# A fused transformer stack: VectorE's statistics cut into single instructions between the scan's steps, PE's and GpSimd's jobs moved to other steps, filler matmuls taken out

## The reference, cut to what matters

```python
def _L0_tok_ref(...):
    emb = tok_table[token_ids] + seg_table[segment_ids] + pos_table[:seq_len][None, :, :]
    ...
    out = (emb - mu) * jax.lax.rsqrt(var + EPS) * gamma + beta

def selective_scan(z, W_xproj, W_dt, b_dt, A_log, D_skip):
    ...
    A_bar = jnp.exp(dt[..., None] * A)
    Bx = (dt * z)[..., None] * Bm[:, :, None, :]
    ...
    _, h = jax.lax.associative_scan(comb, (A_bar, Bx), axis=1)   # h = A_bar * h + Bx along a sequence
    y = jnp.einsum('blds,bls->bld', h, Cm) + D_skip * z

def _L0_attn_ref(x, ...):
    h = rmsnorm(x, w_norm1)
    z = h @ W_in.T
    z = z * jax.nn.sigmoid(h @ W_gate.T)
    y = selective_scan(z, W_xproj, W_dt, b_dt, A_log, D_skip)
    x = residual + y @ W_out.T
    hf = rmsnorm(x, w_ffn_norm)
    return x + jax.nn.silu(hf @ W_gate_ffn.T) * (hf @ W_up.T) @ W_down.T
...
h = _L0_tok_ref(...)
h = h + _L0_attn_ref(_layernorm(h), ...)
h = h + _L0_ffn_ref(_layernorm(h), ...)     # router and 8 experts
```

## Time and profile before

| | us |
|---|---|
| median of three runs | 1750.38 |
| the three runs | 1747.45, 1750.38, 1765.43 |
| the profiled execution, its own time | 1742.62 |
| its span | 1740.9 |
| scan stage in it, first multiply to last scan's end (96.1 to 617.5) | 521.4 |

### The profile page before, as it was taken

The page is one execution under the profiler, slowest core; times in us unless marked ns, Lnnn a source line. Parts: engine busy times, 40 slices in busy tenths (PEclk is TensorE's granted clock), DMA queues, the critical chain, the costliest instruction groups (busy, mean ns, idle before and its releaser), DMA issues.

```text
span 1740.9 us, 23318 instructions
## 1 busy us (share of the span) xinstructions
PE 1355.9 (78%) x7240; PEld 943.2 (54%) x7240; DVE 817.2 (47%) x1505; ACT 520.3 (30%) x878; POOL 519.9 (30%) x418
## 2 busy tenths in 40 slices
PE   0567678889988874699993778989998889998960
PEld 0223333243254453699883554756657488888850
DVE  2478887777688764011112726355453422222212
ACT  0453444764734410133231313315150101001000
POOL 6366644745654471000003400000001600000025
PEclk9978888888798886899997768898988899999985
DMA  5064433433443313889982100000000388888843
GB/s 126 19 167 113 110 89 85 126 98 85 120 105 85 73 53 111 250 274 274 263 260 73 43 1 1 1 1 0 0 1 10 121 226 239 227 233 236 226 128 95
DMA packets 71614, 206.44 MB, mean 119 GB/s; under 512 B 11360, under 2 KB 32608, under 8 KB 66752
## 3 DMA queue, kind: packets, MB, share of 16 engines
q1 hardware_dynamic: 59648, 181.28, 37.9%
q0 software_dynamic: 11904, 24.40, 4.8%
HBM read 183.42 MB, written 22.22 MB: 118 GB/s over the span
## 4 chain that ended last, share of the span: by engine, by line
PE 35%; DMA 24%; DVE 14%; issue 11%; POOL 6%; POOLq 4%; ACT 2%; DVEq 2%; SPq 1%; ACTq 1%
PE ps L825 22%; DMA expert<-arena 21%; PE ps L956 4%; DVE arena L1498 3%; PE ps L1197 3%; POOL arena L545 2%; PE ps L970 1%; PE ps L986 1%; DMA arena<-sorted 1%; DVE ps L1493 1%; POOLq L536 1%; PE ps L1189 1%; POOL ew_out L454 1%; PE ps L820 1%; ACT arena L787 1%
## 5 line engine op out<-in xcount | busy, mean ns | idle before, releaser
L1498 DVE TENSOR_TENSOR_SCAN arena<-arena,ps 128x1024 f32<-128x1024 f32 x96 | 219.6, 2287 | 25.8 <-ACT arena L686 12.8
L825 PE MATMUL ps<-arena 96*128 96x128 f32 (+1 forms) x1680 | 222.8, 290 | 9.9 <-issue 8.3
L825 PEld LDWEIGHTS ps<-arena 96*128 96x128 f32 (+1 forms) x1680 | 213.6, 191 | 14.7 <-issue 14.5
L825 PE MATMUL ps<-xTF,wreg 96*128 96x512 f32 x352 | 207.1, 736 | 8.8 <-DVE arena L1675 5.0
L533 POOL DMA_DIRECT2D expert<-arena x88 | 47.7, 542 | 493.9 <-DVE arena L1635 270.5
L956 PE MATMUL ps<-arena,pick 32*128 32x512 f32 x384 | 124.6, 739 | 86.9 <-DVE arena L1498 75.3
L412 POOL DMA_INDIRECT sorted<-x_rows,row_i x64 | 63.0, 985 | 409.1 <-DVEq L1414 390.4
L825 PE MATMUL ps<-arena,ew_in 96*128 96x128 f32 x1248 | 150.0, 278 | 8.1 <-issue 7.7
L825 PEld LDWEIGHTS ps<-arena,ew_in 96*128 96x128 f32 x1248 | 145.6, 194 | 11.9 <-issue 11.9
L454 POOL TENSOR_TENSOR ew_out<-arena 128x1024 f32<-128x1024 f32 x48 | 112.6, 2351 | 107.4 <-DVE arena L1498 56.6
L1493 DVE TENSOR_TENSOR ps<-ps,arena 128x1024 f32<-128x1024 f32 x96 | 117.2, 1221 | 58.3 <-PE ps L956 56.3
(11 more groups left out here) (213 smaller groups left out, 1867.8 us busy)
## 6 DMA issues: line engine op xcount, KB each, us to landing
arena<-dt SPq DMA_DIRECT2D x64, 512.0 KB, 4.6
ew_in<-in_e_in SPq DMA_DIRECT2D x24, 768.0 KB, 6.1
arena<-in_e_in SPq DMA_DIRECT2D x24, 768.0 KB, 6.1
ew_in<-dt SPq DMA_DIRECT2D x32, 512.0 KB, 4.8
ew_out<-in_e_out SPq DMA_DIRECT2D x20, 675.0 KB, 6.9
arena<-in_e_out SPq DMA_DIRECT2D x20, 675.0 KB, 7.1
ew_in<-in_e_in SPq DMA_DIRECT2D x20, 576.0 KB, 5.5
arena<-in_e_in SPq DMA_DIRECT2D x20, 576.0 KB, 5.6
```

The source lines that it names most:

```text
L825: last = pe.matmul(o, lhs, rhs, start=(n == 0), stop=(n == len(pairs) - 1))
L1498: ve.tensor_tensor_scan(hid[k % 3], dec[k % 3], bx.rearrange("p x t -> p (x t)"), 0.0, ALU.mult, ALU.add)\
```

## The change

The functions `leave_rms` and `leave_norm`, and the calls of `embed_norm` and `embed_rows` in the scan stage, go. The same instructions stand in two new functions. `tile_work` holds what works on whole tiles (`bn_stats`, and the scaling of embedded rows), two tiles at a time behind a scan. `small_work` holds all the rest as 167 pieces of one instruction (`bn_aggr` of four tiles, and one pair, count as one piece); a step has 5 places for pieces in chunks 0 and 3 and 3 in chunks 1 and 2. The first place lies between the multiply and the scan, the others behind the scan; each piece has a `drain` ahead of it. `keep_busy` goes with all its 120 matmuls. The tables of PE's and ScalarE's jobs are written anew, GpSimd's side jobs move to other steps (the residual add from 11, 12 to 5, 6; the embedding of chunks 2 and 3 has a semaphore each and is spread differently), and the bias of the scores of chunk 2 comes behind the loop. The code after the scan stage is the same.

```diff
-        leave_late = {3: [("lnext", 0), ("lnext", 1)], 6: [("lrout", 0)], 7: [("lrout", 1)], 8: [("lscore", 0)]}
+        leave_late = {0: [("ldown", 1)], 8: [("lnext", 0), ("lnext", 1)], 9: [("lrout", 0)], 10: [("lrout", 1)], 11: [("lscore", 0)]}
...
-                    if c and n in (11, 12):
-                        add_mamba(c - 1, n - 11)
+                    if c and n in (5, 6):
+                        add_mamba(c - 1, n - 5)
...
-            def keep_busy(c, n, todo):
...
-                units = 7 - 2 - (2 if n % 2 else 0) - sum(cost[job[0]] for job in todo)
...
-                for _ in range(units):
-                    pe.matmul(ps[:, b, 0:2 * P], ident, cst[:, 0:2 * P], start=True, stop=True)
...
-                keep_busy(c, n, todo)
...
-            def leave_rms(c):
-                ve.wait_ge(s_mr, 2 * (c + 1))
-                moments(mr, CT)
-                rstd(l_rms[:, :], CT, RMS_EPS, True)
-                ve.drain().then_inc(s_rr, 1)
...
+            def root_part(i, o, eps, out):
+
+                v, h, y, t = [w[:, o:o + CT] for w in (vv, vh, yy, tt)]
+                if i == 0:
+                    ve.tensor_scalar(v, mv[:, o:o + CT, 1], eps, None, ALU.add)
+                elif i == 1:
+                    ve.tensor_scalar(ti[:, o:o + CT], v.bitcast(I32), 1, None, ALU.logical_shift_right)
+                    ve.tensor_scalar(h, v, -0.5, None, ALU.mult)
...
+                elif i % 3 == 0:
+                    ve.tensor_tensor(t, y, y, ALU.mult)
...
+            def slots(c):
+                return 3 if c in (1, 2) else 5
+
+            def small_work(c, n, x):
+
+                at = n * slots(c) + x
+                s = slots(c)
...
+                def drained(first, parts):
+                    ve.drain()
+                    return here(first, parts)
+
+                if c == 0:
+                    if here(4, 13) is not None:
+                        embed_norm_part(drained(4, 13))
+                    if here(12, 13) is not None:
+                        embed_norm_part(drained(12, 13))
+                    if here(16, 14) is not None:
+                        embed_rms_part(2, drained(16, 14))
+                    if here(20, 13) is not None:
+                        embed_norm_part(drained(20, 13))
+                if c == 1:
+                    if here(13, 13) is not None:
+                        embed_norm_part(drained(13, 13))
+                    if here(19, 14) is not None:
+                        embed_rms_part(3, drained(19, 14))
+                if c >= 2 and here(3, 14) is not None:
+                    norm_part(c - 2, drained(3, 14))
+                if c and here(6, 15) is not None:
+                    rms_part(c - 1, drained(6, 15))
+                if c == NCH - 1 and here(18, 14) is not None:
+                    norm_part(c - 1, drained(18, 14))
...
                 ve.tensor_tensor(bx, bx, Bt[c % 2].rearrange("p (a t) -> p a t", a=1).broadcast_to((P, 2, CN)), ALU.mult)
                 ve.drain()
+                small_work(c, k % PAIRS, 0)
                 ve.wait_ge(s_dec, 2 * k + 2)
...
                 scan_pair(k)
-                if c and n == 7:
-                    leave_rms(c - 1)
-                if c >= 2 and n == 1:
-                    leave_norm(c - 2)
-                if k == 12:
-                    embed_norm(2, 2)
...
+                for x in range(1, slots(c)):
+                    small_work(c, n, x)
+                tile_work(c, n)
```

More of the change, by code:

```diff
@@ L195, in tower @@
         s_idx, s_sm, s_wa, s_wb = sem("s_idx"), sem("s_sm"), sem("s_wa"), sem("s_wb")
-        s_emb = [sem(f"s_emb{c}") for c in range(3)]
+        s_emb = [sem(f"s_emb{c}") for c in range(4)]
         s_cst, s_neg = sem("s_cst"), sem("s_neg")
@@ L256, in work_at @@
+        rank_at = {14: [("rank", 1)]}
         def work_at(c, n):
-            late = [(what, c - 2, x) for what, x in leave_late.get(n, [])] if c >= 2 else []
+            late = [(what, c - 2, x) for what, x in (late_last if c == NCH - 1 else leave_late).get(n, [])] if c >= 2 else []
             enter = [(what, c + 1, x) for what, x in enter_at.get(n, [])] if c + 1 < NCH else []
@@ L528, in store_blocks @@
+                    if c == NCH - 1 and n in (12, 14):
+                        leave_act(c - 1, n - 12)
+                        leave_act(c - 1, n - 11)
+            add_scores_bias(NCH - 2)
             def store_blocks(m, nb):
@@ L727, in _ @@
                         work(job)
[L728 removed]
+                    if n == 15 and c + 1 < NCH:
                         enter_softplus()
@@ new lines, in gather_part, with rms_part @@
+            def gather_part(o):
+                for j in range(CT):
+                    ve.bn_aggr(mv[:, o + j, :], st[:, o + j, :])
+            def rms_part(c, i):
+                if i == 0:
+                    gather_part(CT)
+                elif i == 1:
+                    ve.tensor_tensor(tt[:, CT:], mv[:, CT:, 0], mv[:, CT:, 0], ALU.mult)
+                elif i == 2:
+                    ve.tensor_tensor(mv[:, CT:, 1], mv[:, CT:, 1], tt[:, CT:], ALU.add)
+                else:
+                    root_part(i - 3, CT, RMS_EPS, l_rms[:, :])
+                if i == 14:
+                    ve.drain().then_inc(s_rr, 1)
@@ new lines, in norm_part, with embed_norm_part @@
+            def norm_part(c, i):
+                if i == 0:
+                    gather_part(0)
+                elif i <= 12:
+                    root_part(i - 1, 0, LN_EPS, n_rstd[:, :])
+                else:
+                    ve.scalar_tensor_tensor(out=n_shift[:, :], in0=mv[:, 0:CT, 0], scalar=-1.0, in1=n_rstd[:, :], op0=ALU.mult, op1=ALU.mult)
+                    ve.drain().then_inc(s_ln, 1)
+            def embed_norm_part(i):
+                if i == 0:
+                    gather_part(0)
+                else:
+                    root_part(i - 1, 0, LN_EPS, n_rstd[:, :])
@@ new lines, in embed_rms_part, with embed_scale @@
+            def embed_rms_part(c, i):
+                if i == 0:
+                    ve.tensor_tensor(tt[:, 0:CT], n_rstd[:, :], n_rstd[:, :], ALU.mult)
+                elif i == 1:
+                    ve.tensor_tensor(mv[:, 0:CT, 1], tt[:, 0:CT], mv[:, 0:CT, 1], ALU.mult)
+                else:
+                    root_part(i - 2, 0, RMS_EPS, x_rms[:, c * CT:(c + 1) * CT])
+                if i == 13:
+                    ve.drain().then_inc(s_rms, 1)
+            def embed_scale(dst, c, j, done=None):
+                for t in (c * CT + j, c * CT + j + 1):
+                    ve.tensor_scalar(dst[:, t, :], h_rows[:, t, :], mv[:, t - c * CT, 0:1], n_rstd[:, t - c * CT:t - c * CT + 1],
+                                     ALU.subtract, ALU.mult)
+                if done is not None:
+                    ve.drain().then_inc(done, 1)
```

192 lines of the change are left out of this document (123 added, 69 removed).

## The result

| | before | after |
|---|---|---|
| median of the runs, us | 1752.64 (1747.45 to 1765.43) | 1806.6 (1796.48 to 1813.28) |
| ratio, 95% interval | | 1.0287 [1.0234, 1.034] |
| profiled execution, us | 1742.62 | 1796.48 |
| scan stage in it, us | 521.4 | 565.1 |
| last scan to the first scatter, us | 4.4 | 10.3 |

The change costs 2.9%. Ratios leave disturbed runs out, so they can differ a little from the quotient of two medians.

A forecast was written before the change was run, and what follows sets the result against it. VectorE was taken to set the pace, waiting for PE after pauses. Floor 341 + VectorE's extras 181 + PE 68 = 590 us of scan stage for 521, so 1819 us, 4% slower; range 1725 to 1885.

The forecast's parts named there:

- Pieces wait out products: In 43 steps, VectorE pieces behind the scan wait for GpSimd's product to end: 88 us, plus 15 for other GpSimd operations.
- The rival that pieces slip past the products: In the 43 steps the 88 us and the 15 go: stage 487, total 1716 us; chance 0.19.
- Pieces, tiles, routing: VectorE's extras in the scan stage: 167 pieces 40 us, tile instructions 16, two routing blocks 15.5.
- Floor: VectorE's multiply-to-multiply pace in the scan stage: 96 steps at 3.55 us, 341 us.
- PE's part: 39 steps with a PE job but neither pieces nor routing, each 1.74 us over the floor: 68 us, bounds 20 and 128.
- Clock: PE's half clock through most light steps and steps with pieces; mean clock in the scan stage under 0.84.
- the rival of a full clock: Clock stays full, waits as forecast, PE part 20 us: stage 542, total 1771 us; chance 0.18.
- PE as the bound: Rival: half clock holds through dense steps too, PE part 128 us: stage 650, total 1879 us; chance 0.17.
- Fillers: Removing 120 matmuls, 74.1 us of PE at the ends of steps' programs, saves little directly: taken as 0.
- Behind the stage: Everything outside the scan stage is unchanged: 1221.2 us stay.

The follow-up runs named there:

- e5: The changed kernel with each piece's instruction replaced by a `bn_aggr`, the norms' factors being constants; 1708.5 us, ratio 0.9814 to the kernel before.
- e9: The changed kernel, no fillers, with all of a step's pieces between its multiply and scan; 1774.7 us, ratio 1.0033 to the kernel before.
- e1: The changed kernel with the 120 filler matmuls put back; 1797.8 us, ratio 1.0332 to the kernel before.
- e10: e9 with the 120 filler matmuls back; 1764.7 us, ratio 1.01 to the kernel before.
- e2: The kernel before with the 120 filler matmuls taken out and nothing else changed; 1767.2 us, ratio 1.0127 to the kernel before.
- e6: The changed kernel, no fillers, each norm's pieces as one block between multiply and scan of its step; 1770.8 us, ratio 1.0028 to the kernel before.
- e4: The changed kernel with each norm's pieces as one block behind the scan and the 120 fillers back; 1774.7 us, ratio 1.0104 to the kernel before.
- e11: e10 with seven pieces to a step, all between multiply and scan; 1748.1 us, ratio 0.9907 to the kernel before.

## Why the prediction was right

- **Pieces wait out products.** The step that decided the sign. Forecast 88 us in the pieces, 15 for other GpSimd operations, 6 in the scalings, 109 in all; counted 81.6, 13.5 and 9.1, with routing 107.4. The picture came as told: 32 of the 41 pieces caught by a product take over 2.2 us, and the multiplies are 6 to 8 us apart in 31 of the 44 steps that hold a piece. e5 shows it by taking the waits away, e9 by moving them. The rival that pieces slip past the products needed 14 or fewer steps caught; in 33 steps a product caught a piece.
- **Pieces, tiles, routing.** Forecast 40 + 16 + 15.5 = 71.5; other extras measured 77.2. I costed the new waits of `bn_stats` for ScalarE's copies at nothing; they wait 15.2 us in the row above, 9.9 of it for ScalarE's copies (10.3 and 4.6 before), so the instructions themselves came out lower.
- **Floor.** 341 forecast at 3.55 us a step, 336.2 measured without the idle time between.
- **PE's part: mis-sized, and not all PE's.** Forecast 68 us, with bounds of 20 and 128; measured 44.4 of idle time ahead of multiplies and scans, of which 20.0 is for PE and 15.3 for ScalarE's decays (the rows of L1642 and L1648 above). The step that failed was carrying the dense stretch's 1.74 us over the floor to all 39 steps with a PE job. That stretch took (65.6 - 13 x 3.55) = 19.5 us over the floor, 1.50 a step. It is luck that this is near 1.74: only 6.6 us of it is VectorE's wait for PE, and 12.2 is for the decays, to which I had given no price ("GpSimd's and ScalarE's moved jobs cost nothing of their own"). The other steps with a job and no pieces have 9.8 us of idle time in all, about 0.4 each; the rest lies in the first step, in the routing steps, in steps with pieces and in steps with none of these. I take it that PE gets ahead in the long steps with pieces; no run separates that.
- **Clock.** Forecast under 0.84, measured 0.73. But its price was wrong in kind: e1, e9 and e10 show that a clock higher by 0.08 to 0.12 changes VectorE's idle time ahead of multiply and scan by under 1 us here, and the stage by 6 to 10 us (e10 against the long execution of e9). In e10 the dense steps ran at 0.97 and took 64.5 us for 65.6. So the rival of a full clock (1771), which put the clock's price at 48 us, had far less to gain. The Trainium skill (TensorE: Matmul & The Clock Gate, "Why this matters for your kernels") asks for no long idle gaps of PE. I had read the change as ending them; it traded 12 pauses for 43 shorter ones with more in sum, and the clock fell. Whether pauses of 3 us are long in the page's sense no run here decides.
- **PE as the bound** fell with the dense stretch: 0.86 in place of 0.79.
- **Fillers.** Taken out at no direct cost: e1 bears that out. In the kernel before they are worth 1.27%, by e2, of which the stage shows 0.5%.
- **Behind the stage: missed.** I took 1221.2 us as unchanged because the code there is. The last PE jobs of the stage were moved to its end and now run after the last scan at the half clock: 5.9 us. With the same tables the gap that was 10.3 us is 7.0 in e1 and 4.0 in e6, so it doesn't hang on the tables alone.

In sum: 590 forecast for the stage, 565.1 measured: PE's part -24, floor -5, waits -2, other extras +6. Outside it +10, of which 5.9 is explained. 1819 forecast, 1806.6 measured: the sign and the waits came by the mechanism, but that the total is so near is in part luck, since the errors inside and outside the stage have opposite signs.

What stays open: how much of the 1% of the re-timed tables (e4) is the cut of the norms into more blocks and how much GpSimd's and ScalarE's new dates, where e11's gain over the kernel before lies beyond the 2.4 us of its stage, and where the 22 us of the fillers in the kernel before lie beyond 8.6.

## What to carry to other kernels

A chain of tiny VectorE instructions on SBUF paid here one GpSimd operation's rest each time it started beside one, so splitting it over more steps bought more waits (53.3 us in 12 blocks, 107.4 in 43 steps); keep it in few groups, or put it where the partner's operation has mostly run (here between the PSUM multiply and the scan), before thinking of PE. Before spreading a block, add up per engine what the pauses cost now (84 us of idle time here) and what each new piece may wait for (43 x 2.35). Fillers for PE's clock are worth what PE's speed is worth at that place: 1.3% in the kernel before, where VectorE waited 56.3 us for PE, nothing that the times show in the changed one, where it waited 20.0.

## What the runs showed of the hardware

- Which VectorE instructions wait for a GpSimd `tensor_tensor` is a matter of the instruction and of where its operands lie, not of its size: a 128x4 `tensor_tensor` in SBUF took 2.36 us beside one, a `bn_aggr` of one tile 0.18, the 128x1024 multiply in PSUM 1.21 to 1.23.
- Starting late doesn't help in kind: begun 1.16 us into the product (125.25 against 124.09), the piece waits to its end at 126.44, 1.21 us.
- The clock can be 0.12 higher (e9 to e10) with no effect on the idle time ahead of multiply and scan, though the statistics then wait 4.9 us less for ScalarE, and 0.10 lower (before to e2) at a price of 1.27%.
